# Taylor attention of a graph network: masked scores kept in fp32 instead of computed twice, on one Trainium2 core

## The reference, cut to what matters

```python
def _L3_gnn_ref(h, adj, w_k, w_q):      # EMB = 8, K_TAYLOR = 4
    h = h - h.mean(axis=-1, keepdims=True)
    h = h / jnp.maximum(jnp.linalg.norm(h, axis=-1, keepdims=True), EPS)
    k = h @ w_k
    q = h @ w_q
    scores = k @ q.T / jnp.sqrt(jnp.float32(EMB))
    a_att = jax.nn.softmax(scores, axis=-1)
    a = adj.astype(jnp.float32) * a_att
    a = a / a.sum(axis=-1, keepdims=True)
    result = a
    fact = 1.0
    for i in range(2, K_TAYLOR):
        a = a @ a
        fact = fact * i
        result = result + a / fact
    return result @ h
```

## Time and profile before

| what | us |
|---|---|
| median of 3 runs | 703.32 |
| lowest and highest of them | 697.76, 705.53 |
| the profiled execution: its own time | 699.14 |
| its span in the trace | 697.1 |
| PE busy, share of the span | 86% |
| DVE, ACT busy | 53%, 37% |
| granted TensorE clock, mean | 0.938 of full speed |

### The profile page before, as it was taken

One profiled execution on the slowest core, in us unless ns is written; L12 is line 12 of the kernel. 1 busy time (PEld: TensorE's weight loads), 2 busy tenths in 40 slices (PEclk: granted clock), 3 DMA queues, 4 the chain that ended last, 5 costly groups with the idle time before them and its releaser, 6 DMA issues.

```text
span 697.1 us, 7544 instructions
## 1 busy us (share of the span) xinstructions
PE 600.4 (86%) x3171; PEld 206.1 (30%) x3171; DVE 370.4 (53%) x523; ACT 257.8 (37%) x267; POOL 30.0 (4%) x27
## 2 busy tenths in 40 slices
PE   5634899978899989899988999986876999999997
PEld 3400122234122344222232222253222233433332
DVE  2663676545767535766646765347986666400001
ACT  1297455432555422545424553512002554200000
POOL 0400000201000100000000000110000000000000
PEclk9755799999999998999999999996998999999999
DMA  8672000000000000000000000000000000000000
GB/s 363 265 313 112 0 1 1 1 0 1 1 1 0 1 1 1 0 1 1 0 1 1 1 1 0 1 1 0 0 1 0 1 0 1 1 0 1 1 0 31
DMA packets 3041, 19.33 MB, mean 28 GB/s; under 512 B 320, under 2 KB 320, under 8 KB 960
## 3 DMA queue, kind: packets, MB, share of 16 engines
q1 hardware_dynamic: 2864, 17.83, 6.3%
q10 hardware_dynamic: 144, 1.03, 0.4%
HBM read 18.33 MB, written 0.52 MB: 27 GB/s over the span
## 4 chain that ended last, share of the span: by engine, by line
PE 69%; DVE 18%; ACT 8%; issue 3%; DMA 1%; POOL 0%; POOLq 0%; DVEq 0%; ACTq 0%
PE PROD L571 13%; PE S L581 8%; PE PROD L781 8%; PE X L781 8%; PE X L563 8%; DVE X L972 5%; DVE aB L1188 5%; ACT big L379 4%; PE X L742 3%; PE X L745 3%; PE X L470 2%; PE M L549 2%; ACT big L339 1%; DVE big L959 1%; DVE aB L964 1%
## 5 line engine op out<-in xcount | busy, mean ns | idle before, releaser
L972 DVE SCALAR_TENSOR_TENSOR X<-wB,v,aB 128x1024 f32<-128x1024 f32 x128 | 161.3, 1289 | 60.3 <-ACT big L339 59.0
L339 ACT ACTIVATE big<-X,v 128x1024 f32<-128x1024 f32 x128 | 137.4, 1112 | 143.3 <-PE X L563 142.9
L571 PE MATMUL PROD<-big,Wh 128*64 128x512 f32 x512 | 126.7, 612 | 1.3 <-ACT big L339 0.9
L563 PE MATMUL X<-nadj,bigI 128*128 128x512 bf16 x256 | 72.1, 387 | 26.6 <-DVE X L972 26.5
L581 PE MATMUL S<-big,onesf 128*32 128x512 f32 x512 | 68.2, 605 | 0.0
L571 PEld LDWEIGHTS PROD<-big,Wh 128*64 128x64 f32 x512 | 30.2, 136 | 80.7 <-ACT big L339 50.9
L742 PE MATMUL X<-nadj,bigI 128*128 128x512 bf16 x128 | 41.8, 411 | 11.4 <-DVE aB L1188 8.2
L563 PEld LDWEIGHTS X<-nadj,bigI 128*128 128x128 bf16 x256 | 16.0, 97 | 103.6 <-DVE X L972 76.4
L1188 DVE TENSOR_TENSOR aB<-aB,X 128x1024 f32<-128x1024 f32 x32 | 39.1, 1220 | 4.6 <-PE X L745 3.4
L745 PE MATMUL X<-wB 96*128 96x512 bf16 (+1 forms) x128 | 40.7, 400 | 0.0
L549 PE MATMUL M<-big,level 128*32 128x512 fp8e4 x256 | 20.8, 437 | 19.9 <-ACT big L379 16.8
(11 more groups left out here) (243 smaller groups left out, 513.8 us busy)
## 6 DMA issues: line engine op xcount, KB each, us to landing
big<-in_adjT SPq DMA_DIRECT2D x16, 1024.0 KB, 8.0
cst<-in_cst ACTq DMA_DIRECT2D x1, 1008.5 KB, 5.6
x<-in_xT SPq DMA_DIRECT2D x1, 512.0 KB, 6.2
out<-x SPq DMA_DIRECT2D x2, 256.0 KB, 2.0
```

The source lines that it names most:

```text
L339: act.activation(prob[:, t % U, :], X[t % 2][:], ACT.Exp, bias=v2[l % 2][:, k:k + 1]).then_inc(p_ready, 1)
L563: last = pe.matmul(X[t % 2][:, hh * BANK:(hh + 1) * BANK], bigI[:], nadj[:, k, half_cols(c, hh)], start=False, stop=True, skip_group_check ...
L571: pe.matmul(PROD[c][feat(hh), :], Wh[l % 2][:, k, :], prob[:, t % U, hh * BANK:(hh + 1) * BANK], start=k == 0, stop=k == NB - 1)
L972: dve.scalar_tensor_tensor(X[t % 2][:], wB[:, cols(c)], v8[l % 2][:, k:k + 1], aB[:, cols(c)], ALU.max, ALU.add).then_inc(x_written, 1)
```

## The change

The scores are computed once. ScalarE copies each PSUM tile of masked scores unchanged into `att[c]` in fp32 (`stored`, semaphore `s_stored`, which now frees the buffer `X`). VectorE takes the running maximum from `att` in SBUF (`maxima`). The maximum of each target is found as before (`max_columns`, `column_max`), negated, and spread to all 128 partitions by fp32 matmuls with a broadcast column (`lower_rows`, then `lower_row` copies it over `accf`). VectorE adds this row to each stored tile in place (`lowered`, semaphore `s_lowered`), and ScalarE takes the exponential in place (`attention`). TensorE multiplies each tile by the features (`absorb`, `propagate`) and, for every two tiles, adds up the columns by four 32-wide fp32 matmuls with ones into `S`. `totals_copy` takes `S` to SBUF, and `row_totals` uses the constant `pick` on it. The steps of the two chunks are interleaved: chunk 1's tile `k` is scored, stored and compared in the same turn of each engine's loop in which chunk 0's tile `k - 5` (`LAG`) is lowered, exponentiated and multiplied. The three further applications are as before, but the products are turned in `X[0]` and `M`.

The diff, without the declarations of semaphores and blank lines:

```diff
--- before.py
+++ after.py
@@ -64,7 +64,6 @@
         accf = aB
-        rowsum = aB[:].rearrange("p (c n) -> p c n", c=NCH)
         row3 = sb("row3", [PARTS, CH], bf16)
...
@@ -133,7 +132,7 @@
         vm = sb("vm", [P, CB])
-        m3 = sb("m3", [P, CB, PARTS], bf16)
+        sT = sq[:, 1, :]
         seed = sb("seed", [P, 2])
...
@@ -209,14 +208,16 @@
...
@@ -227,6 +228,11 @@
...
+        TURN = [(PROD[0], PROD[1]), (M, PROD[1])]
+        LOWER = [(M, S), (M, PROD[1])]
+        LAG = 5
+        back = [X[0][:, BANK:CH], M[:]]
         block = ctx.enter_context(nc.Block())
...
@@ -411,15 +417,26 @@
             kq_rows(1)
-            def max_row(c):
-                act.wait_ge(mrow_psum, c + 1)
-                act.activation(KQ[KPAD:KPAD + PARTS, c, 0, :], (M, S)[c][:].bitcast(bf16)[0:PARTS, :],
-                               ACT.Copy).then_inc(mrow_ready, 1)
+            def stored(c, k):
+                s = NB * c + k
+                act.wait_ge(s_ready, s + 1)
+                act.activation(att[c][:, k, :], X[s % 2][:], ACT.Copy).then_inc(s_stored, 1)
+            def lower_row(c):
+                act.wait_ge(low_psum, c + 1)
+                for b in range(2):
+                    act.activation(accf[:, half_cols(c, b)], LOWER[c][b][:], ACT.Copy).then_inc(low_ready, 1)
             def attention(c, k):
-                s = NB * c + k
-                act.wait_ge(s_ready, NCH * NB + s + 1)
-                act.activation(att[c][:, k, :], X[k % 2][:], ACT.Exp).then_inc(a_ready, 1)
+                act.wait_ge(s_lowered, NB * c + k + 1)
+                act.activation(att[c][:, k, :], att[c][:, k, :], ACT.Exp).then_inc(a_ready, 1)
+            def totals_copy(c):
+                act.wait_ge(a_summed, c + 1)
+                if c:
+                    act.wait_ge(rowsum_psum, c)
+                act.activation(sT, S[:], ACT.Copy).then_inc(rowsum_ready, 1)
             def reciprocal_copy(c):
...
@@ -429,19 +446,30 @@
                 new = Y[q % 2][:, CB * c:CB * (c + 1), :].rearrange("p (h b) f -> p b h f", h=2)
-                act.activation(new, (S, M)[n % 2][:].rearrange("p (b h f) -> p b h f", b=HB, h=2),
+                act.activation(new, back[n % 2].rearrange("p (b h f) -> p b h f", b=HB, h=2),
                                ACT.Copy).then_inc(y_ready, 1)
-            max_row(0)
-            max_row(1)
             for k in range(NB):
+                stored(0, k)
+            for k in range(NB):
+                stored(1, k)
+                if k == LAG - 1:
+                    lower_row(0)
+                if k >= LAG:
+                    attention(0, k - LAG)
+            for k in range(NB - LAG, NB):
                 attention(0, k)
+                if k == NB - 3:
+                    lower_row(1)
             for k in range(NB):
                 attention(1, k)
-                if k == 7:
+                if k == 2:
+                    totals_copy(0)
+                if k == 6:
                     reciprocal_copy(0)
-                if k == 11:
+                if k == 10:
                     turned(0)
+            totals_copy(1)
             reciprocal_copy(1)
...
@@ -737,43 +765,34 @@
             key_rows(1)
-            def score(s, c, jb, depth):
+            def score(s):
+                c, jb = s // NB, s % NB
+                if s >= 2:
+                    pe.wait_ge(s_stored, s - 1)
                 for hh in range(2):
...
                     last = pe.matmul(X[s % 2][:, hh * BANK:(hh + 1) * BANK],
-                                     KQ[0:depth, jb // CB, 1, (jb % CB) * P:(jb % CB + 1) * P],
-                                     KQ[0:depth, c, 0, hh * BANK:(hh + 1) * BANK], start=False, stop=True)
+                                     KQ[0:KPAD, jb // CB, 1, (jb % CB) * P:(jb % CB + 1) * P],
+                                     KQ[0:KPAD, c, 0, hh * BANK:(hh + 1) * BANK], start=False, stop=True)
                 last.then_inc(s_ready, 1)
...
                 for b in range(CB):
-                    last = pe.transpose(PROD[b // HB][:, (b % HB) * P:(b % HB + 1) * P],
+                    last = pe.transpose(TURN[c][b // HB][:, (b % HB) * P:(b % HB + 1) * P],
                                         accf[:, c * CH + b * P:c * CH + (b + 1) * P], ident)
                 last.then_inc(maxT_psum, 1)
-            def max_rows(c):
-                pe.wait_ge(m3_ready, c + 1)
+            def lower_rows(c):
+                pe.wait_ge(vm_ready, c + 1)
                 for b in range(CB):
-                    last = pe.transpose((M, S)[c][:].bitcast(bf16)[0:PARTS, b * P:(b + 1) * P], m3[:, b, :], identb[:])
-                last.then_inc(mrow_psum, 1)
-            pe.wait_ge(kT_ready, 2 * NCH)
-            pe.wait_ge(y0_ready, NCH)
-            for s in range(NCH * NB):
-                if s >= 2:
-                    pe.wait_ge(max_done, s - 1)
-                score(s, s // NB, s % NB, KPAD)
-                if s == NB + 2:
-                    max_columns(0)
-                if s == NB + 8:
-                    max_rows(0)
-            max_columns(1)
-            max_rows(1)
-            pe.wait_ge(mrow_ready, NCH)
+                    last = pe.matmul(LOWER[c][b // HB][:, (b % HB) * P:(b % HB + 1) * P], vm[:, b:b + 1].broadcast_to([P, P]),
+                                     ident, start=True, stop=True)
+                last.then_inc(low_psum, 1)
             def propagate(out, c, src, jb):
@@ -782,10 +801,26 @@
                 return last
+            def absorb(c, k):
+                pe.wait_ge(a_ready, NB * c + k + 1)
+                last = propagate(PROD[c], c, Y[1], k)
+                if k == NB - 1:
+                    last.then_inc(q_psum, 1)
+                if k % 2 == 0:
+                    return
+                if c and k == 1:
+                    pe.wait_ge(rowsum_ready, c)
+                for strip in range(4):
+                    tile, hh = k - 1 + strip // 2, strip % 2
+                    last = pe.matmul(S[32 * strip:32 * strip + 32, :], onesf[:, 0:32],
+                                     att[c][:, tile, hh * BANK:(hh + 1) * BANK], start=k == 1, stop=k == NB - 1)
+                if k == NB - 1:
+                    last.then_inc(a_summed, 1)
             def row_totals(c):
                 pe.wait_ge(rowsum_ready, c + 1)
-                for b in range(CB):
-                    last = pe.matmul((M, X[0])[c][:, b:b + 1], rowsum[:, c, b * P:(b + 1) * P], onesf[:, 0:1],
+                for bb in range(HB):
+                    last = pe.matmul((M, X[0])[c][:, 2 * bb:2 * bb + 2], sT[:, bb * P:(bb + 1) * P], pick,
                                      start=True, stop=True)
...
@@ -793,7 +828,7 @@
                 for b in range(CB):
-                    hh, bb = b // HB, b % HB
+                    hh, bb = b % 2, b // 2
                     col = rec8[:, b:b + 1].broadcast_to([P, F])
...
@@ -804,26 +839,34 @@
                 for bb in range(HB):
-                    last = pe.transpose((S, M)[n % 2][:, bb * P:(bb + 1) * P], z[n % 2][:, bb * P:(bb + 1) * P], ident)
+                    last = pe.transpose(back[n % 2][:, bb * P:(bb + 1) * P], z[n % 2][:, bb * P:(bb + 1) * P], ident)
                 last.then_inc(zT_psum, 1)
-            for s in range(2):
-                score(NCH * NB + s, 0, s, KPAD + PARTS)
-            for c in range(NCH):
-                for k in range(NB):
-                    s = NB * c + k
-                    pe.wait_ge(a_ready, s + 1)
-                    last = propagate(PROD[c], c, Y[1], k)
-                    if k == NB - 1:
-                        last.then_inc(q_psum, 1)
-                    if s + 2 < NCH * NB:
-                        score(NCH * NB + s + 2, (s + 2) // NB, (s + 2) % NB, KPAD + PARTS)
-                    if c and k == 2:
-                        row_totals(0)
-                    if c and k == 5:
-                        spread_totals(0)
-                    if c and k == 9:
-                        turn(0)
+            pe.wait_ge(kT_ready, 2 * NCH)
+            pe.wait_ge(y0_ready, NCH)
+            for s in range(NB):
+                score(s)
+            for k in range(NB):
+                score(NB + k)
+                if k == 1:
+                    max_columns(0)
+                if k == 3:
+                    lower_rows(0)
+                if k >= LAG:
+                    absorb(0, k - LAG)
+            max_columns(1)
+            for k in range(NB - LAG, NB):
+                absorb(0, k)
+                if k == NB - 4:
+                    lower_rows(1)
+            for k in range(NB):
+                absorb(1, k)
+                if k == 3:
+                    row_totals(0)
+                if k == 5:
+                    spread_totals(0)
+                if k == 9:
+                    turn(0)
             row_totals(1)
...
@@ -1166,29 +1209,28 @@
             first_rows(1)
-            dve.memset(accf[:], -BIG).then_inc(accf_clear, 1)
```

(59 more changed lines are left out.)

10 lines of the change are left out of this document (6 added, 4 removed).

## The result

| | before | after |
|---|---|---|
| median of the runs, us | 701.09 (4 runs, 697.76 to 705.53) | 760.54 (4 runs, 758.11 to 763.28) |
| profiled execution, us | 699.14 | 758.11 |
| its span, us | 697.1 | 756.3 |
| granted TensorE clock, mean | 0.938 | 0.88 |

The ratio of after to before is 1.0826, with a 95% interval of 1.0768 to 1.0885: slower by 8%.

What follows compares the result with a forecast made beforehand. It took a circle of waits through in-order queues to bound the middle loop: sixth maximum at 515.5 us, loop to 610.0, then 15 + 26 + 3.7 to 654.7, 49 later than before; 748, taken as 749, range 727 to 763.

Steps and rivals of the forecast that it cites:

- fully cold: Rival: all ten loop steps at 9.6 us and slow restarts of TensorE behind the loop, 760 us; chance 0.08.
- (4): After the loop: 15 us for the remaining lowerings and exponentials, then chunk 1 bound by TensorE, 26 us.
- The circle: Middle loop, k = 5 to 15: in-order queues make each engine's step wait for another's, so nothing runs side by side.
- Price of a turn: One middle-loop turn: 6.8 us, 7.8 with sums, at 2.4 GHz; 8.6 and 10.6 at 1.2 GHz.
- Ten steps: Middle loop from k = 5 to k = 15: 9.2 us each at a mostly cold clock, 92 us.
- full clock: Rival: the waits close but TensorE keeps 2.4 GHz in the loop, 73 us there, 730 us in all; chance 0.16.
- (1): Chunk 0 stored and compared, from the first score at 479.67 us: ends at 503.6.
- (2): From chunk 0's last maximum to chunk 1's sixth: transposes, spreading, scores and copies, 11.9 us, none hidden.
- (5): From the last sums to the further applications: totals copy, row totals, reciprocal, spreading and handovers, 3.7 us.
- Memory: Rival: three engines sharing tiles in SBUF; steps slower by a tenth add 5 us in the loop; no separate chance.
- Side by side: Rival: a score can pass products queued ahead, so loop turns cost VectorE's 2.47 us; 682 us in all; chance 0.05.

Runs made afterwards that it cites:

- fourteen fillers: Changed kernel plus fourteen matmuls, results unread, on TensorE between score and wait for the exponential in each turn with an old tile: 742.91 us.
- staggered kernel: Changed kernel with TensorE's old tile two tiles later (k - 7), ScalarE's one later (k - 6), VectorE's unchanged: 690.09 us, 0.981 of before.

## Why the prediction was right

I forecast 749 us in a range of 727 to 763, slower; it is 760.5, near the upper end. The mechanism is the one that I described. That the time equals the 760 of the rival "fully cold" is chance: the loop was not fully cold (a clock of 0.61, 91.8 us), and of the 5 to 10 us that this rival gave to (4), 2.1 came. What is above my sum lies mostly elsewhere. Its steps, one by one:

- *The circle* was right. Every handover of the predicted order is in the timeline of after, and taking one step out of it (TensorE, then ScalarE, then the sums) changed the turn by what that step had cost, or, for the sums, the five turns that held them.
- *Price of a turn* was right at both clocks: 8.6 and 10.6 us forecast at the 1.2 GHz level, 8.52 and 10.38 measured (three of the five turns with sums were shorter, 9.18 to 9.70, their ends being at full clock, as I had expected of some); 6.8 and 7.8 at 2.4 GHz, 6.78 and 7.76 measured in the run with fourteen fillers. The exponential from SBUF was 1.056 us (1.05 taken), the copy 1.023 (1.025), the operations from SBUF 1.225.
- *Ten steps*: 92 us forecast, 91.8 measured. The mean clock was 0.61, so the rivals "full clock" (73 us) and "fully cold" (96 us) both fall, the second by little.
- *Chunk 0 and the way to the sixth maximum of chunk 1*, (1) and (2): 35.8 us from the first score forecast, 37.2 measured. The granted clock was 0.71 and 0.72 from 508 to 516, where the spreading by fp32 matmuls and the score behind it lie, and I had priced both at full clock: the spreading took 2.5 us (512.30 to 514.77), not 1.1. (The terms of (2) add up to 11.8, not the 11.9 written there.)
- *The last part*, (4) and (5), is the term that was mis-sized: 44.7 us forecast from the end of the last lowering inside the loop, 51.2 measured (613.8 to 665.0). It has two causes. The first is an order of queues that I left out: I had priced the totals, spreading and turn of chunk 0 as 3.3 us of TensorE and nothing else, but they stand in VectorE's queue ahead of lowerings. `row_reciprocals(0)` waits 4.97 us for the totals, the lowerings behind it come late, and TensorE waits for their exponentials 1.47 us, then 0.79 and 0.62, 2.9 us in all. The staggered kernel shows this part alone: at a clock of 1.00 it has the same three waits, and from its first products of chunk 1 to its last sums it takes 29.0 us, where I had 26. The second cause is the clock. After took 30.6 us for the same piece (630.9 to 661.5); its clock was 0.57 from 640 to 644, so the products and sums there took 3.6 us (640.18 to 643.74) instead of 2.0. And (4), which I had at 15 us, took 17.1 (613.8 to 630.9) at a clock of 0.83: the first products and the transposes took 1.9 us each (614.98 to 618.78) instead of 1.0 and 1.1. The first cause is the mistake that I had warned of in the loop, made once more: the work was counted, and not what is queued behind the wait for it.
- The first score came 2.7 us later than in the profile before, which no step of mine speaks of. With 1.4 from (1) and (2) and 6.5 from (4) and (5), and 0.5 less in the loop and the further applications, this is the distance between my sum, 748, and the profiled 758.1.
- *Memory*: no operation was slower for three engines using the tiles; VectorE's 30 maxima from SBUF took 1.224 to 1.226 us. (A tile is 512 KB, 4 KB in each partition, and not 64 KB as I wrote; 64 KB a partition is the whole of `att[c]`.)
- *Side by side*: the rival's mechanism, had the circle been open, is what the staggered kernel shows, 26.65 us for ten steps where I had 25. Its sum of 682 us was 8 us short of the run's 690, but not for the last part, which took 45.1 us against 44.7, with two tiles more: this trace's first score starts at 487.02 instead of 479.67, 7.3 us later, and the way to the loop and the loop itself took 3 us more.

## What to carry to other kernels

When two chains are interleaved over several engines with in-order queues, write down one turn and follow the waits: if every engine does "new step, then old step", the old step of one turn and the new step of the next form a circle through all engines, and the distance in tiles doesn't open it (at LAG 9 a turn still took 9.1 us). Give each engine further down the chain one turn more of distance, or don't interleave; here that was worth 70 us in 760. And when a step with a wait is placed or moved, ask in each queue what stands behind it, the copies that free a buffer among them.
